# Input gates of a GRU quad: four chunks of 384 columns become three of 512

## The reference, cut to what matters

```python
def cell(h, x):                      # 64 steps, batch B = 32, width 512
    gi = x @ W_ih + b_ih             # 512 -> 3 * 512: the input gates, no state in them
    gh = h @ W_hh + b_hh             # needs the state of the step before
    i_r, i_z, i_n = jnp.split(gi, 3, axis=-1)
    h_r, h_z, h_n = jnp.split(gh, 3, axis=-1)
    r = jax.nn.sigmoid(i_r + h_r)
    z = jax.nn.sigmoid(i_z + h_z)
    n = jnp.tanh(i_n + r * h_n)
    return (1.0 - z) * n + z * h
x = x + gru(cond_2048, x)            # all 64 states
x = x + attention_over_8_blocks(x)   # small; a few us at the end of the kernel
```

## Time and profile before

| | us |
|---|---|
| median of 3 runs | 384.88 (381.39 to 385.06) |
| the profiled execution's own time | 382.3 |
| its span | 380.5 |
| TensorE busy | 363.2 (95%) |
| VectorE busy | 261.8 (69%) |
| ScalarE busy | 159.3 (42%) |
| mean granted TensorE clock | 0.991 of full speed |

### The profile page before, as it was taken

How to read it: one execution, slowest core, us unless ns; L and a number is a source line. 1 busy time by engine, 2 the same in 40 slices (tenths; PEclk the granted TensorE clock), 3 DMA queues, 4 the chain that set the end, 5 groups by cost and what they waited for, 6 DMA issues and landing times.

```text
span 380.5 us, 9825 instructions
## 1 busy us (share of the span) xinstructions
PE 363.2 (95%) x3281; PEld 213.9 (56%) x3281; DVE 261.8 (69%) x1134; ACT 159.3 (42%) x506; POOL 20.2 (5%) x53
## 2 busy tenths in 40 slices
PE   7999999999999999999999999999999999996873
PEld 4466555566666555556666655556666654334552
DVE  2735667687676767786768676867777676778675
ACT  4712326262625343434435262626262556582300
POOL 7011000000000000000000000000000001000120
PEclk9999999999999999999999999999999999999898
DMA  5975535423232323232232414142323222101056
GB/s 180 399 287 118 163 88 162 115 51 97 72 97 69 97 69 95 70 73 72 69 96 56 109 46 106 35 114 50 97 69 97 69 69 72 29 28 29 3 203 239
DMA packets 27484, 38.63 MB, mean 102 GB/s; under 512 B 2988, under 2 KB 19016, under 8 KB 27464
## 3 DMA queue, kind: packets, MB, share of 16 engines
q1 hardware_dynamic: 27432, 38.36, 34.8%
q10 hardware_dynamic: 32, 0.01, 0.0%
HBM read 18.17 MB, written 4.19 MB: 59 GB/s over the span
## 4 chain that ended last, share of the span: by engine, by line
PE 89%; DVE 5%; issue 2%; DMA 1%; POOL 1%; SPq 1%; POOLq 0%; ACT 0%; DVEq 0%
PE gates_ps L595 42%; PE gi_ps L563 36%; DMA h_tok<-hist 1%; DVE gcx L1090 1%; PE first_ps L595 1%; PE first_ps L656 1%; PE fourth_ps L595 1%; PE third_ps L595 1%; PE keys_ps L595 1%; PE fourth_ps L656 1%; PE third_ps L656 1%; PE keys_ps L656 1%; POOL w_hh L367 1%; PE gi_ps L577 0%; PE keys_ps L721 0%
## 5 line engine op out<-in xcount | busy, mean ns | idle before, releaser
L595 PE MATMUL gates_ps<-w_hh,turned 128*32 128x384 f32 x1920 | 167.3, 489 | 0.5 <-DVE turned L808 0.5
L595 PEld LDWEIGHTS gates_ps<-w_hh,turned 128*32 128x32 f32 x1920 | 56.4, 109 | 85.6 <-issue 56.4
L563 PE MATMUL gi_ps<-w_ih_hi,xt_hi 128*128 128x384 f32 x240 | 87.2, 363 | 0.0
L563 PE MATMUL gi_ps<-w_ih_hi,xt_lo 128*128 128x384 f32 x240 | 81.2, 338 | 0.0
L563 PE MATMUL gi_ps<-w_ih_lo,xt_hi 128*128 128x384 f32 x240 | 80.2, 334 | 0.0
L477 ACT ACTIVATE rz<-gates_ps 128x256 f32<-128x256 f32 x60 | 23.1, 385 | 128.9 <-PE gates_ps L595 128.8
L870 DVE TENSOR_TENSOR rz<-gates_ps,rz 128x128 f32<-128x128 f32 x60 | 17.5, 292 | 80.4 <-ACT rz L477 80.4
L563 PEld LDWEIGHTS gi_ps<-w_ih_hi,xt_hi 128*128 128x128 f32 x240 | 45.0, 187 | 37.5 <-issue 37.5
L563 PEld LDWEIGHTS gi_ps<-w_ih_lo,xt_hi 128*128 128x128 f32 x240 | 45.1, 188 | 0.0
L563 PEld LDWEIGHTS gi_ps<-w_ih_hi,xt_lo 128*128 128x128 f32 x240 | 45.0, 187 | 0.0
L808 DVE STREAM_TRANSPOSE turned<-hist 128x32 f32<-128x32 f32 (+1 forms) x192 | 36.7, 217 | 2.2
(11 more groups left out here) (218 smaller groups left out, 302.1 us busy)
## 6 DMA issues: line engine op xcount, KB each, us to landing
gi<-gi_tok SPq DMA_DIRECT2D x60, 192.0 KB, 3.4
x1t<-in_x_t_dram SPq DMA_DIRECT2D x16, 256.0 KB, 3.2
gcx<-in_x_tok_dram SPq DMA_DIRECT2D x16, 256.0 KB, 3.2
h_tok<-hist SPq DMA_DIRECT2D x64, 64.0 KB, 2.2
out_dram<-gcx SPq DMA_DIRECT2D x16, 256.0 KB, 2.1
gcx<-in_w_ih_dram SPq DMA_DIRECT2D x4, 768.0 KB, 8.0
w_hh<-in_w_hh_dram SPq DMA_DIRECT2D x4, 768.0 KB, 8.5
wo_t<-in_wo_t_dram SPq DMA_DIRECT2D x1, 1024.0 KB, 5.4
```

Of the source, the lines that this page charges most:

```text
L563: mm = pe.matmul(gi_ps[tok][:, 0:G3], a[:, k, :], w[:, k, gi_cols(j)], start=(k == 0 and a is xt_hi and w is w_ih_hi), stop=(k == NJ - 1 a ...
L595: mm = pe.matmul(gates_bank(t)[j * B:(j + 1) * B, P:], before[:, k * B:(k + 1) * B], chunk(w_hh, k, j), start=False, stop=(k == NJ - 1), s ...
```

## The change

The 1536 columns are cut into three chunks of 512 instead of four runs of 384. A chunk is again 12 matmuls (four blocks of the contraction, three products), now with 512 columns, so a quad has 36 matmuls instead of 48, and as many columns in all (36 x 512 = 48 x 384). They are spread as nine behind each of the four steps, and so a chunk begins and ends within a step's share: behind steps 4q - 5 to 4q - 2 stand the matmuls 0 to 8, 9 to 17, 18 to 26 and 27 to 35 of quad q, and the chunks end with 11, 23 and 35. VectorE keeps a chunk of 512 columns in each of the first three steps of a quad and none in the fourth. The chunk borders no longer fall on the borders of the groups of partitions, so each chunk is moved by two DMAs (`gi_pieces`): 384 + 128 columns, 256 + 256, and 128 + 384. A quad has six moves in place of four. The seed L416 for step 4q waits for all six.

```diff
--- before.py
+++ after.py
@@ tiles
-        gi_tok = sb("gi_tok", [P, 2, G3])
+        gi_tok = sb("gi_tok", [P, 2, D])
...
@@ helpers
+        def gi_pieces(c):
+
+            return (((0, 0, G3, 0), (1, 0, P, G3)), ((1, P, G3, 0), (2, 0, 2 * P, 2 * P)),
+                    ((2, 2 * P, G3, 0), (3, 0, G3, P)))[c]
+
+        def chunk_of(i, s):
+
+            return i * 6 + 3 * (s // Q) + s % Q
+
+        def uses_of(i, s):
+
+            return i * 3 + (3 * (s // Q) + s % Q) // 2
@@ SyncE
             def move_gi(i, s):
 
-                idx, pos = i * S + s + 5, s + 5
-                q, j = i * 2 + pos // Q, pos % Q
-                slot, tok = (pos // Q) % 2, pos % 2
-
-                wait(sp, gi_tok_ready, idx + 1 - Q)
-
-                if j == 0 and not (isinstance(q, int) and q < 3):
+                q, c = i * 2 + s // Q + 1, s % Q
+                slot, tok = (s // Q + 1) % 2, chunk_of(0, s) % 2
+
+                wait(sp, gi_tok_ready, chunk_of(i, s) + 1)
+
+                if c == 0 and not (isinstance(q, int) and q < 3):
                     wait(sp, x1t_ready, q - 1)
-                sp.dma_start(gi[j * B:(j + 1) * B, slot, :], gi_tok[:, tok, :]).then_inc(gi_moved[tok], 16)
+                for j, lo, hi, at in gi_pieces(c):
+                    rows = gi[j * B:(j + 1) * B, slot, :].rearrange("p (t c) -> p t c", t=Q)
+                    sp.dma_start(rows[:, :, lo:hi], gi_tok[:, tok, at:at + hi - lo]).then_inc(gi_moved[tok], 16)
...
-                    if not (last and i * S + s + 5 >= T):
+                    if s % Q < Q - 1 and not (last and s >= Q):
                         move_gi(i, s)
...
-            move_gi(0, -1)
@@ ScalarE
-                wait(act, gi_done, (quad - 1) * Q)
+                wait(act, gi_done, (quad - 1) * 3)
...
                 if s % Q == 0:
 
-                    for tok in range(2):
-                        wait(act, gi_moved[tok], (i * 2 + s // Q) * 32)
+                    for tok, uses in enumerate(((0, 0), (2, 1), (3, 3))[s // Q]):
+                        wait(act, gi_moved[tok], (i * 3 + uses) * 32)
@@ TensorE
-            def gi_chunk(idx, pos, quad):
-
-                tok, j = pos % 2, pos % Q
-                if j == 0:
+            def gi_part(quad, slot, number):
+
+                if number == 0:
 
                     wait(pe, x_lo_ready, quad)
-
-                wait(pe, gi_tok_ready, idx - 1 - Q)
-                for k in range(NJ):
-                    for a, w in ((xt_hi, w_ih_hi), (xt_hi, w_ih_lo), (xt_lo, w_ih_hi)):
-                        mm = pe.matmul(gi_ps[tok][:, 0:G3], a[:, k, :], w[:, k, gi_cols(j)],
-                                       start=(k == 0 and a is xt_hi and w is w_ih_hi),
-                                       stop=(k == NJ - 1 and a is xt_lo))
-                mm.then_inc(gi_done, 1)
+                for m in range(9 * number, 9 * number + 9):
+                    c, (j, term) = m // 12, divmod(m % 12, 3)
+                    tok = (slot * 3 + 3 + c) % 2
+                    a, w = ((xt_hi, w_ih_hi), (xt_hi, w_ih_lo), (xt_lo, w_ih_hi))[term]
+                    if m % 12 == 0:
+
+                        wait(pe, gi_tok_ready, quad * 3 - 3 + c - 1)
+                    mm = pe.matmul(gi_ps[tok][:], a[:, j, :], w[:, j, c * D:(c + 1) * D], start=(m % 12 == 0),
+                                   stop=(m % 12 == 11))
+                    if m % 12 == 11:
+                        mm.then_inc(gi_done, 1)
...
-                if not (last and t + 5 >= T):
-                    gi_chunk(t + 5, s + 5, i * 2 + (s + 5) // Q)
+                if not (last and s >= Q - 1):
+                    q = s // Q + (s + 1) // Q - s // Q + 1
+                    gi_part(i * 2 + q, q % 2, (s + 1) % Q)
...
-            gi_chunk(Q, Q, 1)
+            gi_part(1, 1, 0)
@@ VectorE
-            def keep_gi(idx, pos):
-
-                tok, j = pos % 2, pos % Q
-
-                wait(dve, gi_done, idx + 1 - Q)
-                wait(dve, gi_moved[tok], (idx - tok - Q) * 8)
-                dve.tensor_tensor(gi_tok[:, tok, :], gi_ps[tok][:, 0:G3], b_in[:, gi_cols(j)],
+            def keep_gi(i, s):
+
+                tok, c = chunk_of(0, s) % 2, s % Q
+
+                wait(dve, gi_done, chunk_of(i, s) + 1)
+                wait(dve, gi_moved[tok], uses_of(i, s) * 32)
+                dve.tensor_tensor(gi_tok[:, tok, :], gi_ps[tok][:], b_in[:, c * D:(c + 1) * D],
                                   ALU.add).then_inc(gi_tok_ready, 1)
...
-                if peeled and s == 0:
-                    dve.wait_ge(b_in_ready, 1)
-                    keep_gi(Q, Q)
                 if peeled and s < Q - 1:
-                    dve.wait_ge(b_in_ready, s + 2)
+                    dve.wait_ge(b_in_ready, (1, 3, 4)[s])
...
-                if not (last and t + 5 >= T):
-                    keep_gi(t + 5, s + 5)
+                if tt < Q - 1 and not (last and s >= Q):
+                    keep_gi(i, s)
```

More of the change, by code:

```diff
@@ L75, in gru_block_attention @@
         br_turned, br_cur = sb("br_turned", [P, P]), sb("br_cur", [P, P])
-        br_all = sb("br_all", [P, NB * P])
-        br_t = sb("br_t", [P, NJ, NB * B])
+        br_all = sb("br_all", [P, (NB - 1) * P])
+        br_t = sb("br_t", [P, NJ, (NB - 1) * B])
         x_mean = sb("x_mean", [P, NQ])
@@ L355, in _ @@
                 save_block(i - 1)
-            pool.wait_ge(gi_tok_ready, T - Q)
+            pool.wait_ge(gi_tok_ready, 3 * (NQ - 1))
             pool.tensor_tensor(gmask, gamma_rec[:, None, :].broadcast_to([P, NJ, P]),
@@ L552, in _ @@
         def _(pe):
-            def gi_chunk(idx, pos, quad):
-                tok, j = pos % 2, pos % Q
-                if j == 0:
+            def gi_part(quad, slot, number):
+                if number == 0:
                     wait(pe, x_lo_ready, quad)
-                wait(pe, gi_tok_ready, idx - 1 - Q)
-                for k in range(NJ):
-                    for a, w in ((xt_hi, w_ih_hi), (xt_hi, w_ih_lo), (xt_lo, w_ih_hi)):
-                        mm = pe.matmul(gi_ps[tok][:, 0:G3], a[:, k, :], w[:, k, gi_cols(j)],
-                                       start=(k == 0 and a is xt_hi and w is w_ih_hi),
-                                       stop=(k == NJ - 1 and a is xt_lo))
-                mm.then_inc(gi_done, 1)
+                for m in range(9 * number, 9 * number + 9):
[8 more added lines that the diff above has]
+                        mm.then_inc(gi_done, 1)
             def keys(group, part):
                 if part == 0:
-                    pe.wait_ge(gi_tok_ready, T - 1 - Q + group)
+                    pe.wait_ge(gi_tok_ready, 3 * (NQ - 1) - group)
                     pe.wait_ge(wk_in, 16)
```

## The result

The kernel with three chunks takes 392.27 us, median of four runs (391.15 to 393.77); the kernel before took 384.24 us beside it (381.39 to 385.06). The ratio is 1.0225, with a 95% interval from 1.0159 to 1.0291: 2.25% slower. The prediction was 393 us, range 387 to 398.5. The profiled execution took 393.77 us, its span was 391.9, against 382.3 and 380.5 before. It is the slowest of its four, and 382.3 lies under the median before, so the two traces differ by more (11.4 us) than the medians (8.0).

The account below looks back on a forecast made before the run. TensorE, alternating recurrence and input gates every 5.02 us, was taken as the bound; 15 x 0.78 - 45 x 0.05 = +9.4 us gave 391.7 on the profiled execution, 394.3 on the median; predicted 393 us, range 387 to 398.5.

Parts of the forecast that it names:

- the second issue: SyncE, third step of a quad: the large move, issued behind the small one, starts 0.65 us later, at least 0.55.
- the slack: Between the end of a quad's first seed and TensorE's start: of 0.25 us, 0.05 taken as free.
- the landing: Last chunk's large move: lands 3.3 us after its issue, as the moves of before, at best near 2.1 to 2.9.
- A step's phase: TensorE's input gates, every step: nine 512-column matmuls replace twelve of 384, 2.30 to 2.25 us; bounds 0.00 and 0.13 less.
- the upper end of 0.233: Cost of a 512-column matmul if the streaming rate is what is lower: 233 ns, and nothing gained.
- The Trainium skill's distance: TensorE by the skill's gap: 512 columns cost 216 ns, a step gains only 8 ns, the sum becomes +10.7 us.
- `keep_gi`, +0.13: VectorE's read of 512 PSUM columns takes about 0.69 us, 0.13 more each, three a quad in place of four.
- The "faster" rival: Large move lands under 2.6 us after issue and matmuls cost 216 ns: all 60 intervals gain 0.13, 374.5 us; chance 0.05.
- A held interval: Interval ahead of each quad's first step: 0.73 us late plus the lost step gain of 0.05, so +0.78 over 5.02.
- The sum: Whole kernel: 15 held intervals lose 0.78 us, 45 gain 0.05, +9.4 us in all; +7.1 to +11.0 at the bounds.
- What would show it: Profile after: matmuls 0.228 us apart, TensorE idle 0.7 to 0.8 once a quad, recurrences 5.8 apart there, 4.97 elsewhere.
- the bank's wait: TensorE's extra wait for a bank within a step's share: worth nothing; a hole from it was part of "worse still", chance 0.08.

Follow-up runs that it names:

- experiment 6: Three-chunk kernel with each 512-column matmul split into two of 256 with the same weights (values don't hold): 394.42 us, ratio 1.0312 to the kernel before.
- experiment 4: Three-chunk kernel, last chunk's large move issued before the small one and its 384 columns also kept first by VectorE: 385.3 us, ratio 1.0068 to the kernel before.
- Experiment 2: Kernel before, with each quad's last run moved as 128 + 256 columns by two transfers: 383.61 us, ratio 1.004 to the kernel before.
- experiment 7: Three-chunk kernel with chunks as gates r, z, n, twelve 64 KB moves a quad, seed waiting for r and z alone: 379.83 us, ratio 0.9912 to the kernel before.
- experiment 5: Kernel before, with 2 of each quad's last run's 384 columns moved by a 1 KB transfer ahead of the other 382: 389.98 us, ratio 1.0169.
- Experiment 1: Three-chunk kernel without the small move of each quad's last chunk from step 8 on (seeds read old values): 384.3 us, ratio 1.0035 to the kernel before.
- experiments 3: Three-chunk kernel with the last chunk's large move issued ahead of the small one: 387.82 us, ratio 1.0134 to the kernel before.

## Why the prediction was right

It was right in sign, in size and by its mechanism. That 393 lies within 1 us of the median is in part luck: it was counted half on a median before of 384.88 that more runs put at 383 to 384.2, and in the sum terms that were off one way (the second issue 0.05 us too long, the slack 0.07 too small) stand against terms off the other way (the landing and the hand-overs, 0.04 each). Step by step:

- **A step's phase, 0.05 us less.** Measured 0.04. The matmul costs 0.230, between the 0.228 taken and the upper end of 0.233; experiment 6 shows that the choice (the cost beyond the columns is fixed) held for some 10 of its 17 ns.
- **The Trainium skill's distance.** By the Trainium skill, "TensorE: Matmul & The Clock Gate", section "Back-to-back issue gap", 512 columns would be 216 ns apart. The section gives N / 2.4 + 2.5 as the gap of isolated matmuls, and 131 ns for 512 columns in a stream of load and matmul, which the prediction left out. The trace has 230, as it had 175 and not 162 for 384, and agrees with neither; the rows were the better ground.
- **`keep_gi`, +0.13.** 684 ns on the page, for 551; experiment 4 got 0.14 of it back.
- **The second issue, +0.65.** It was 0.60. The rows I used were of the four transfers of the states; two moves of gi stand 0.60 apart.
- **The landing, 3.3.** 3.36, with 192 KB. The "faster" rival asked for a second landing under 2.6 us. Experiment 2 shows that such a thing comes near (2.8), but from a smaller transfer, not from its place as the second.
- **The slack, 0.05.** This term was mis-sized: it is 0.11 to 0.13. All of 0.25 less the 0.12 of the shortest way in the loop was free; the 0.20 of the earlier trace rows wasn't that way's least.
- **A held interval, +0.78 over 5.02.** Measured 0.69 to 0.75 in most, 0.73 on average. With the sizes above, the landing 0.04 later and the step's gain of 0.04: 0.13 + 0.60 + 0.04 + 0.04 - 0.12 = 0.69. The 0.04 left over is spread over the hand-overs between the engines.
- **The sum, +9.4.** The profiled execution stood at +11.5 (393.77 against 382.3). The terms that were foreseen give 12.0 - 1.4 - 1.5 = 9.1; 1.4 came from the two long issues, 0.2 from the start and 0.8 from the end of the kernel, which the prediction had at nothing. The medians differ by 8.0.
- **What would show it.** Matmuls 0.230 apart, 4.98 elsewhere and 5.7 to 5.8 once a quad, 0.72 us idle ahead of the recurrence: all as told. That the bank's wait stays off the path is shown by experiment 7, which has it and loses nothing.

Experiment 2 was a miss of the same reasoning used too freely: I carried the price of a second issue over to a case where the transfer behind it had become smaller.

**The long issues.** They stand in every kernel, and the traces show what goes with them. Behind the first 25 us the nine traces have 39 issues on SyncE of more than 0.75 us, and each one ends 0.34 to 0.41 us behind the end of a 16 KB transfer of the kind `instruction` on queue 8. The two of the kernel after: such transfers from 60.25 to 61.57 and from 330.30 to 331.34, the issues' ends at 61.96 and 331.73. The first of them in the DMA queues' rows of 60 to 62 us (packets, MB, share of 16 engines):

```profile
q8 instruction: 1, 0.02, 4.1%
```

From 104 to 300 us, in the later turns of the loop, no trace has such a transfer, and none has a long issue. So it is likely that SyncE waits there for its own code; no run tests it. In the kernel before, the long issues fell on two loads of x and one move of the states, for which nobody waits. Experiment 2's one interval over 5.02 (5.89 us) is one of them, and experiment 5's longest (6.74). A kernel whose seed hangs on the end of the queue pays for them, one with slack doesn't.

**What stays open** is the 0.8 us at the end. The granted clock falls to 0.50 (1.2 GHz) there in both traces, at different places: three groups of four matmuls (L699, before L683) take 0.85 us each at 0.50 after and 0.44 before at full clock, while before the 32 matmuls of the keys (L721) fell into it (1.78 us, 1.08 after). Experiment 1, with the same instructions there as the kernel after, takes 40.48 us, less than the kernel before, so it need not be the change. Nor need the 0.2 us of the start: step 1 starts between 27.83 and 28.41 in the experiments.

## What to carry to other kernels

Before a transfer is cut in two, find who waits for its last part: the cut costs one issue (0.6 us here) less what the smaller last part lands sooner, and nothing at all where the consumer has that much slack. Fewer and longer matmuls gain only their fixed cost, here 0.04 us a step for three matmuls fewer; a single wait on a DMA can take back nearly twenty times that. Where pieces must arrive late, order them by first use, so that the last to land is the last to be read; this turned 2% lost into 0.9% gained.

## What the runs showed of the hardware

- **The landing goes by size, with a large fixed part.** From SyncE's issue: 1 KB 1.74 us, 64 KB 2.1, 128 KB 2.8, 192 KB 3.35, each alone or behind a smaller one. The Trainium skill, "DMA: Bandwidth & Descriptors", section "Anatomy of one DMA — SWDGE (gpsimd) path", gives about 2.0 us and bytes / 436 GB/s for transfers that GpSimd issues; by it an estimate for 192 KB is 2.45 us, which the trace's 3.35 doesn't agree with. For these, issued by SyncE from tile to tile in pieces of 512 to 1536 bytes, the measured slope between 64 and 192 KB is 1.25 us for 128 KB, some 105 GB/s, and the fixed part is under 1.74.
- **A transfer behind a larger one is slower.** 64 KB take 3.06 us behind 192 KB, and 2.1 ahead of them.
- **An issue of these moves on SyncE is 0.55 us, 0.60 for the next in a row**, whatever their size: 547 ns for 1 KB too. It isn't the same for every transfer: the loads of x (256 KB from memory) have issues of 0.41 in the median.
- **Now and then an issue takes 0.8 to 1.8 us**, behind the first 25 us always with the end of an instruction transfer 0.3 to 0.4 us before its own. A large move lands as much later (4.30 instead of 3.36); 64 KB behind 192 KB land at 3.06 to 3.21 all the same, as experiments 3 and 4 have it at steps 8 and 60.
- **A float32r matmul at 2.4 GHz costs its columns and 13 to 17 ns** (0.120, 0.175 and 0.230 us for 256, 384 and 512). The first matmuls of the kernel before stand 0.43 us apart with 512 columns, which is 1.2 GHz with nothing beyond; the trace has no record of the clock before 8.3 us, so the level there is read from the distance.
